# A two-layer gated attention and feed-forward kernel: attention's last six x tiles turned by DMA instead of TensorE, and four small moves in the order

## What is computed

```
x = x + tanh(g_xattn[0]) * long_conv(ctx, ctx, layernorm(x), taps, D, 8)
x = x + tanh(g_ffn[0])   * ffn_ternary(layernorm(x), w1, w2, w3)      # 512 -> 1408 -> 512
x = x + tanh(g_xattn[1]) * attention(layernorm(x), ctx, mask)
x = x + tanh(g_ffn[1])   * ffn_one_bit(layernorm(x), w1, w2, w3)      # 512 -> 2048 -> 512

attention: scores = (x @ ctx.T) / sqrt(512), masked, softmax, readout = attn @ ctx
```

## Time and profile before

| what | us |
|---|---|
| median of 3 runs | 694.18 (693.56 to 695.19) |
| the profiled execution's own time | 692.84 |
| its span (first to last instruction) | 691.0 |
| PE busy | 682.8 (99%) |
| DVE busy | 580.3 (84%) |
| ACT busy | 410.4 (59%) |
| POOL busy | 294.8 (43%) |
| mean granted TensorE clock | 0.999 of 2.4 GHz |

### The profile page before, as it was taken

How to read it: one execution, slowest core, us unless ns; L and a number is a source line. 1 busy time by engine, 2 the same in 40 slices (tenths; PEclk the granted TensorE clock), 3 DMA queues, 4 the chain that set the end, 5 groups by cost and what they waited for, 6 DMA issues and landing times.

```text
span 691.0 us, 9572 instructions
## 1 busy us (share of the span) xinstructions
PE 682.8 (99%) x3162; PEld 389.0 (56%) x3162; DVE 580.3 (84%) x1054; ACT 410.4 (59%) x630; POOL 294.8 (43%) x455
## 2 busy tenths in 40 slices
PE   9999999999999999999999999999999999999997
PEld 7777777777444444567754444444444444444445
DVE  4999998999899998658957889988898888898891
ACT  4679899857679898657677354423434423434440
POOL 5889999999765554537401421111110011110000
PEclk9999999999999999999999999999999999999999
DMA  8896664653479989897140243354333233342244
GB/s 297 261 284 184 224 188 133 152 149 104 128 150 198 185 179 206 219 365 278 19 134 17 61 107 76 76 93 92 76 92 39 68 92 92 78 75 63 62 69 114
DMA packets 155377, 94.64 MB, mean 137 GB/s; under 512 B 133825, under 2 KB 134337, under 8 KB 155329
## 3 DMA queue, kind: packets, MB, share of 16 engines
q1 hardware_dynamic: 153600, 90.02, 51.4%
q0 software_dynamic: 1200, 3.93, 1.7%
q10 hardware_dynamic: 528, 0.09, 0.1%
HBM read 53.04 MB, written 8.47 MB: 89 GB/s over the span
## 4 chain that ended last, share of the span: by engine, by line
PE 86%; DVE 6%; POOL 4%; DMA 2%; issue 1%; ACT 1%; SPq 0%; POOLq 0%; ACTq 0%
PE psum L875 29%; PE psum L724 16%; PE psum L907 15%; PE psum L802 9%; PE psum L814 5%; PE psum L858 4%; PE psum L836 4%; POOL phase_space L576 1%; DMA phase_space<-in_taps 1%; PE psum L891 1%; PE psum L825 1%; DVE phase_space L1422 1%; DVE phase_space L1355 1%; PE psum L720 1%; DVE phase_space L1249 1%
## 5 line engine op out<-in xcount | busy, mean ns | idle before, releaser
L875 PE MATMUL psum<-phase_space 128*128 128x512 f16 x1024 | 223.8, 379 | 0.1
L875 PEld LDWEIGHTS psum<-phase_space 128*128 128x128 f16 x1024 | 100.0, 98 | 122.2 <-issue 1.7
L724 PE MATMUL psum<-phase_space 128*128 128x288 f32 x640 | 158.6, 407 | 1.4 <-POOL phase_space L579 1.4
L724 PEld LDWEIGHTS psum<-phase_space 128*128 128x128 f32 x640 | 120.3, 190 | 33.6 <-POOL phase_space L579 1.9
L703 POOL DMA_DIRECT2D out<-x_sb x15 | 9.3, 621 | 234.7 <-DVE x_sb L1431 234.7
L907 PE MATMUL psum<-phase_space 128*128 128x512 f16 x480 | 105.7, 379 | 0.0
L1196 ACT ACTIVATE phase_space<-psum,b_scalars 128x512 f32<-128x512 f32 x64 | 43.5, 682 | 75.1 <-PE psum L875 74.9
L1202 ACT ACTIVATE phase_space<-phase_space,magic 128x1024 f32<-128x1024 f32 x32 | 36.5, 1150 | 77.3 <-DVE phase_space L1415 77.3
L802 PE MATMUL psum<-phase_space 128*128 128x512 bf16 (+1 forms) x384 | 79.0, 361 | 0.7 <-DVE phase_space L1297 0.4
L907 PEld LDWEIGHTS psum<-phase_space 128*128 128x128 f16 x480 | 47.0, 98 | 56.6
L1400 DVE SCALAR_TENSOR_TENSOR phase_space<-psum,b_scalars,phase_space 128x512 f32<-128x512 f32 x64 | 47.7, 748 | 28.3 <-ACT phase_space L1196 28.3
(11 more groups left out here) (123 smaller groups left out, 1071.6 us busy)
## 6 DMA issues: line engine op xcount, KB each, us to landing
phase_space<-in_L_weights SPq DMA_DIRECT2D x24, 512.0 KB, 6.1
phase_space<-in_L_weights SPq DMA_DIRECT2D x12, 704.0 KB, 6.8
phase_space<-kpad SPq DMA_DIRECT2D x14, 512.0 KB, 4.2
phase_space<-in_context_heads SPq DMA_DIRECT2D x15, 384.0 KB, 4.8
x_sb<-in_x_tiles SPq DMA_DIRECT2D x16, 256.0 KB, 4.6
phase_space<-in_context_turned SPq DMA_DIRECT2D x8, 512.0 KB, 6.0
x_between<-x_sb SPq DMA_DIRECT2D x16, 256.0 KB
x_sb<-x_between SPq DMA_DIRECT2D x16, 256.0 KB, 6.9
```

Source lines behind the costliest of these rows:

```text
L724: return nc.tensor.matmul(at(bank(4 * hh + lo), 0, [[64, B], [1, NP]]), toep[n % 2][:, hh, (lo - li) * P:(lo - li + 1) * P], kv[n % 2][:, ...
L875: last = nc.tensor.matmul(bank(2 * (m % 3) + w), fb_qT[n % 2][:, kk % 2, kk // 2, :], b_wT[w][:, kk // 2, c * 512:(c + 1) * 512], start=(k ...
```

## The change

- **Attention's x by DMA.** For tiles 10 to 15 `c_turn_x` and the copy from PSUM go. POOL, after the norm, splits the row in two planes of 16-bit halves (two `tensor_scalar` of 512 columns, new in `c_norm`), SP issues one DMA transpose of 128 x 1024 16-bit words (`turn_rows`, new), and ACT joins the halves from `at_turned` to `at_xT` (two activations of 512 columns instead of one). Planes and turned rows have two buffers each; one transpose waits for the one before it to land. In SP's list turn_rows(10) stands ahead of load_b(19), and turn_rows(11) to (15) behind it and ahead of the next stage's first turn.
- **Low halves.** `fb_low_x` of tiles 0, 1 and 2 goes from DVE to POOL (`fb_low_early`): (0) and (1) behind c_norm(14) and c_norm(15), (2) behind the loop. DVE's later steps get waits for them.
- **pairs(1)** goes ahead of the third tile's root on POOL.
- **a_round_h(0)** goes on ACT from ahead of a_silu(1, 1) to behind it.
- **`ones`** is set ahead of `ident`, and the warm-up waits for it alone.

```
@@ -152,6 +152,8 @@
         at_xh = fa_xh
+        at_planes = [view(off, [2 * L], BF16).bitcast(U16) for off in (R_F + 9728, R_A + 7680)]
+        at_turned = [view(R_F + k * L, [2 * LB, P], BF16).bitcast(U16) for k in range(2)]
 
@@ -324,11 +326,18 @@
         NBA = 11
+        BY_DMA = 10
         SIGN_STEP = {0: 11, 3: 12, 5: 13, 6: 14, 7: 15, 8: 16, 13: 17, 15: 18}
...
         NEG_STEP = {4: 0, 6: 1, 8: 2, 10: 3}
+
+        def c_normed(i):
+            return i + 1 if i < BY_DMA else BY_DMA + 2 * (i + 1 - BY_DMA)
+
+        def c_turned(i):
+            return i + 1 if i < BY_DMA else BY_DMA + 16 * (i + 1 - BY_DMA)
 
@@ -504,8 +513,18 @@
                 reload(15)
-                for j in range(17, 20):
-                    load_b(j)
+                def turn_rows(i):
+                    sp.wait_ge(c_xt, c_turned(i - 1))
+                    sp.wait_ge(c_xh, c_normed(i))
+                    sp.wait_ge(c_xe, i - 1)
+                    sp.dma_start_transpose(at_turned[i % 2], at_planes[i % 2]).then_inc(c_xt, 16)
+
+                load_b(17)
+                load_b(18)
+                turn_rows(10)
+                load_b(19)
+                for i in range(11, NT):
+                    turn_rows(i)
 
@@ -619,11 +638,25 @@
                     ln_root(pool, 2, i)
-                    if i >= 2:
+                    if i < 2:
+                        pool.wait_ge(f_q, NT)
+                    elif i < BY_DMA + 2:
                         pool.wait_ge(c_xt, i - 1)
-                    else:
-                        pool.wait_ge(f_q, NT)
                     ln_norm(pool, 2, i, at_xh[i % 2], c_xh)
+                    if i >= BY_DMA:
+                        pool.wait_ge(c_xh, c_normed(i) - 1)
+                        if i >= BY_DMA + 2:
+                            pool.wait_ge(c_xt, c_turned(i - 2))
+                        src = at_xh[i % 2].bitcast(U16)
+                        for half in range(2):
+                            last = nc.gpsimd.tensor_scalar(at_planes[i % 2][:, half * L:(half + 1) * L], at(src, half, [[2, L]]),
+                                                           1.0, 0.0, ALU.mult, ALU.add)
+                        last.then_inc(c_xh, 1)
+
+                def fb_low_early(n):
+                    pool.wait_ge(g_hi, n + 1)
+                    nc.gpsimd.tensor_tensor(fb_qp[n % 2][:, 1, :], fb_q[n % 2], fb_qp[n % 2][:, 0, :], ALU.subtract
+                                            ).then_inc(g_lo, 1)
 
@@ -631,8 +664,8 @@
 
+                nc.gpsimd.memset(ones[:, :], 1.0).then_inc(s_const, 1)
                 nc.gpsimd.memset(ident[:, :], 0.0).then_inc(s_const, 1)
-                nc.gpsimd.memset(ones[:, :], 1.0).then_inc(s_const, 1)
                 nc.gpsimd.memset(magic[:, 0:1], MAGIC).then_inc(s_const, 1)
@@ -642,10 +675,12 @@
                 for n in range(3):
+                    if n == 2:
+                        pairs(1)
                     ln_root(pool, 0, n)
...
                 for n in range(NT):
-                    if n + 1 < NT:
+                    if 1 <= n < NT - 1:
                         pairs(n + 1)
@@ -691,6 +726,9 @@
                         b_norm(i - 8)
+                    if 12 <= i < 14:
+                        fb_low_early(i - 12)
+                fb_low_early(2)
                 for n in range(3):
@@ -731,7 +769,7 @@
                 def warm_up():
-                    pe.wait_ge(s_const, 2)
+                    pe.wait_ge(s_const, 1)
                     for _ in range(12):
@@ -936,7 +974,7 @@
                         turn_p(i - 1)
-                    if 1 <= i < NT - 1:
+                    if 1 <= i < BY_DMA - 1:
                         c_turn_x(i + 1)
@@ -1082,11 +1120,18 @@
                 def c_copy_x(i):
-                    act.wait_ge(c_xt, i + 1)
+                    act.wait_ge(c_xt, c_turned(i))
                     if i >= 2:
...
                         act.wait_ge(f_up, 3 * NT)
+                    if i >= BY_DMA:
+                        src = at_turned[i % 2].rearrange("p k c -> p (k c)")
+                        dst = at_xT[i % 2].rearrange("p k c -> p (k c)").bitcast(U16)
+                        for half in range(2):
+                            last = nc.scalar.activation(at(dst, half, [[2, L]]), src[:, half * L:(half + 1) * L], ACT.Copy)
+                        last.then_inc(c_xe, 1)
+                        return
                     nc.scalar.activation(at_xT[i % 2], bank4(i % 2), ACT.Copy).then_inc(c_xe, 1)
@@ -1156,9 +1201,11 @@
                     a_silu(t, 0)
-                    if t >= 1:
+                    if t >= 2:
                         a_round_h(t - 1)
                     a_silu(t, 1)
+                    if t == 1:
+                        a_round_h(0)
                     if 1 <= t < NT - 2:
@@ -1373,6 +1420,8 @@
                         dve.wait_ge(g_hi, n - 1)
+                    if 2 <= n < 5:
+                        dve.wait_ge(g_lo, n - 1)
                     nc.vector.tensor_tensor(grouped(fb_q[k]), grouped(fb_xh[k]), spread(fb_gx[k][:, 2, :], NGX), ALU.mult
@@ -1391,6 +1440,8 @@
                     dve.wait_ge(g_hi, n + 1)
+                    if n == 3:
+                        dve.wait_ge(g_lo, 3)
                     nc.vector.tensor_tensor(fb_qp[n % 2][:, 1, :], fb_q[n % 2], fb_qp[n % 2][:, 0, :], ALU.subtract
@@ -1543,8 +1594,6 @@
                         fb_deq_x(i - 10)
-                    if 12 <= i < 14:
-                        fb_low_x(i - 12)
                     if i == 13:
@@ -1587,8 +1636,6 @@
                         b_residual(n - 3)
-                    if n == 0:
-                        fb_low_x(2)
                     if 3 <= n < NT - 2:
```

## The result

The changed kernel takes **696.62 us** in the median of 7 runs (695.58 to 697.28); the kernel before took 693.56 in the 7 runs beside it (693.03 to 695.44). The ratio is 1.004, with an interval of 1.0029 to 1.0050: slower by 0.4%. The profiled execution took 696.83 for a span of 695.0, 4.0 longer than the span before. The kernel before has two kinds of executions: of its 82 runs beside the experiments 21 show a mean granted clock of 0.996 or 0.997 and take 694.8 to 695.8, and nearly all the others take 692.7 to 693.9, so its median moves by some tenths with the mix.

What follows compares the result with a forecast made beforehand. PE was taken to bound the kernel, with POOL's list deciding in attention. Terms +3.1 - 1.4 - 0.1 = +1.6, put on the median 694.18, gave 695.8 us, slower by 0.23%; range 692.0 to 698.0.

Steps and rivals of the forecast that it cites:

- PE alone, -2.6 over six rounds: Attention: six rounds of 4.10 each lose PE's turn of 0.44, -2.6 if everything else follows.
- ACT's join: Attention: copy of 0.60 becomes two activations, some 1.15; next scores start at about 3.9 in the round, not 3.66.
- POOL's planes at 0.62: Attention: each of POOL's two new passes per tile takes 0.62, bounds 0.31 and 0.79; 1.50 a tile with overheads.
- Term +3.1: Attention: POOL's late planes of tile 15 put scores(15) at 350.0 against 346.9; bounds -0.7 and +5.1.
- The clock rival, 0.05: Attention: PE's waits drop the granted clock to 1.2 GHz for one round, 3.7 more, 699.5; chance 0.05.
- Term -1.4 at the start: First convolution products: pairs(1) moved earlier on POOL removes PE's 1.40 wait at 17.19; bounds 0 and -1.4.
- a_round_h, -0.1: PE's 0.44 wait at 184.15 goes, but the next down product waits for its transpose: -0.1, bounds 0 and -0.44.

Runs made afterwards that it cites:

- the filler's run: Changed kernel plus nine 128-column products of ones by ones, result unread, on PE ahead of scores(14): 695.74 us.
- With DVE mended: Changed kernel with all turns on PE, and POOL waiting for DVE's first 32x1 addition before pairs(1): 692.88 us, against 692.95 without the wait.
- the last kernel: Changed kernel with all turns on PE, POOL's wait at the start, and copy_result(0) directly behind the join of tile 3's planes: 691.24 us.

## Why the prediction was right, and where its steps were not

The time was forecast at 695.8, slower by 0.2%, and is 696.62, slower by 0.4%, inside the range. Of the +3.1 (medians of the runs side by side), +1.6 was foreseen. The time looks nearer than the change does, because the sum was put on 694.18, and the kernel before took 693.56 beside the changed one. Step by step:

- **PE alone, -2.6 over six rounds, if all else follows.** Right: two rounds of 3.66 appear as soon as ACT joins first.
- **ACT's join.** I put 1.15 for two activations, by the split's 0.62, and rounds of 3.9. They measure 763 ns each and 1.39 a pair, and rounds of 3.97. The split reads with a stride of two and writes in one piece; the join does the reverse. The mechanism was right, the size 0.24 short. It could have been read: the trace of before has a nearer row than the split, the convolution's own join (`join_q`), with the same 763:

```profile
L1001 ACT ACTIVATE phase_space<-phase_space 128x512 uint16<-128x512 uint16 x28 | 21.4, 763 | 9.6 <-DMA phase_space<-phase_space 9.0 <-issue 0.5
```

- **POOL's planes at 0.62.** The group shows 1.20 a pair. POOL reached tile 15's last plane at 344.91, forecast 345.9, without a gap: a tile with its planes took 3.40 (321.56 to 324.96), forecast 3.63.
- **Term +3.1.** The mechanism was right: POOL's list is late, and its order alone gives back 3.7. The step that failed is the place, and with it what follows: tile 15 was to set scores(15). It was tile 14, whose transpose took 3.4 to land and not 2.8, and then the clock. Tiles 10 and 11 were to "come just in time" and stalled PE for 0.56 and 0.72, with landings of 3.4 and 4.6; before scores(13) and (15) PE did not wait. Without the lowered clock the loss is 27.5 - 24.7 = 2.7 (the filler's run). That this is near the forecast is in part chance, since other stalls make it up. The clock brings it to 4.3 in the profiled execution.
- **The clock rival, 0.05.** This happened, by the mean clocks in four of seven runs, at 1.2 to 1.6 and not 3.7. The price failed because the low clock covered less work than the 3.66 of a round: scores(14) alone here, parts of scores(14) and of the readout in the run with the low halves on DVE. What I held against it, the 1.40 at the start, was a shorter stall than the 2.42 that my own sum had nearly given: 0.3 to 3 us in three rounds. The Trainium skill (TensorE: Matmul & The Clock Gate, Part 1: The HAM clock gate) says that idle stretches bring the lower level back. Here the trace agrees for 2.42 and 2.63, and shows a full clock behind 1.18 and 1.78. The trace of before did have an example, behind its last matmul: PE ends at 686.6, the clock is full up to 689, and 0.53 over 689 to 691.
- **Term -1.4 at the start.** Wrong: -0.2. "DVE, slowed by POOL's pairs beside its products, is late with them" stood in the forecast's spread only; it happened in every trace with pairs(1) in its new place and no wait, and on the folds, not the products (1.21 and 0.96 as before, one operand in PSUM). And a second step failed: the late root "feeds only the products of tile 2, one whole convolution tile further on". It feeds the planes of tile 2, and through the transposes a copy that PE waits for at 37.8. With DVE mended, the gain was still 0.1.
- **a_round_h, -0.1.** Right: 0.44 of waiting became 0.70, and PE came to the first down product 0.15 earlier.

So the verdict came out right with two errors on the same side, a start that did not gain (1.2) and a clock that fell (4.25 - 2.7 = 1.5 in the profiled execution), and 0.4 off the attention term on the other. From +1.6 they lead to 1.6 + 1.2 + 1.5 - 0.4 = 3.9, against the 4.0 between the two spans. Without the two the same sum is 1.2, or 0.17%, less than what can be told from no change: the mechanism in attention was right, but that the kernel came out visibly slower is luck.

## What to carry to other kernels

A low busy share says nothing about an engine that works through a fixed list: POOL was 44% busy and made the whole loss, because steps with a late deadline stood ahead of steps with an early one. When a wait is removed, follow every step that was moved behind it to its last reader, across engines and queues, not only to the next use; here a root of 0.55 us came back as 1.7 on PE 20 us later. And before an order is given up as slow, mend it engine by engine: the same DMA part went from 3.7 us dearer than PE's turns to 1.7 cheaper.

## What the runs showed of the hardware

- VectorE operations with both operands in SBUF slow down several times beside GpSimd's products of two SBUF operands: two folds of 128x128 from 0.62 to 1.63, an addition of 32x1 from 0.15 to 1.06, and one of 128x512 from 0.69 to 1.56. The slowdown goes both ways: GpSimd's own last pair goes from 0.72 to 1.17 in such company, and a `tensor_tensor` of 128x1 from 0.55 to 1.02 where VectorE's addition had begun first. In the last kernel, where both began at 16.37, it took 0.55. VectorE's operations with an operand in PSUM did not change (0.95 to 0.96 and 1.20 to 1.23).
- An activation over 512 16-bit words takes 763 ns where it reads in one piece and writes with a stride of two (L1132, and L1001 in the kernel before), and 624 ns the other way round.
- A transpose of 128x1024 16-bit words, SBUF to SBUF, lands 2.7 to 4.8 after its issue. The slowest, 4.5 to 4.8 in five kernels, had a load of 512 KB ahead of it in the queue; with that load behind it, it took 3.6.
- The granted clock fell behind idle times of 2.42 and 2.63 us, once with the first products and once a microsecond into the work, and stayed at 0.50 up to 348.5 and 350.0, some 3 us of work in each. It cost 1.6 in the profiled execution of the changed kernel. It does not happen each time: three of the seven runs of that kernel show no drop in their mean clock.
